# A two-layer transformer block with experts on one core: layer 0's second routing and layer 1's weight fold move into the first expert blocks

## What is computed

```
x = x + tanh(g_xattn[0]) * xattn0(layernorm(x), ctx)          # 16 heads
x = x + tanh(g_ffn[0])   * ffn0(layernorm(x))                 # layer 0's experts:
    scores = softmax(xt @ Wg + bg);  topk_probs, topk_idx = top_k(scores, 2)
    h  = gelu(xt @ W1[e] + b1[e]);   eo = h @ W2[e] + b2[e]
    out = sum over the two experts of topk_probs * eo
x = x + tanh(g_xattn[1]) * xattn1(layernorm(x), ctx)          # 1 head, causal
x = x + tanh(g_ffn[1])   * ffn1(layernorm(x))                 # experts pick tokens
```

## Time and profile before

| | |
|---|---|
| time, 3 runs | median 1029.1 us (1027.45 to 1030.93) |
| the profiled execution | 1028.68 us, of which 1026.9 us are the span of the trace |
| PE | 913.3 us busy, 89% of the span |
| DVE, ACT, POOL | 605.3, 532.7 and 680.3 us busy |
| granted TensorE clock, mean | 0.966 of full speed |

### The profile page before, as it was taken

The page is one execution under the profiler, slowest core; times in us unless marked ns, Lnnn a source line. Parts: engine busy times, 40 slices in busy tenths (PEclk is TensorE's granted clock), DMA queues, the critical chain, the costliest instruction groups (busy, mean ns, idle before and its releaser), DMA issues.

```text
span 1026.9 us, 24961 instructions
## 1 busy us (share of the span) xinstructions
PE 913.3 (89%) x8860; PEld 765.9 (75%) x8860; DVE 605.3 (59%) x1600; ACT 532.7 (52%) x1258; POOL 680.3 (66%) x905
## 2 busy tenths in 40 slices
PE   5999997797739999999999989978998999999991
PEld 3777775565528989999989978865776767778881
DVE  6888889987964563245625769984635324433320
ACT  2666765465415446444644666635555445545440
POOL 6565657588747777376427777721786658878885
PEclk9999999899869999999999999998999999999996
DMA  9364433022145756676456663131364644575454
GB/s 370 119 204 162 154 128 124 17 74 67 51 171 178 216 174 203 209 214 190 157 180 190 196 239 105 58 111 43 53 85 47 114 47 51 84 102 56 50 57 44
DMA packets 130154, 130.73 MB, mean 127 GB/s; under 512 B 32882, under 2 KB 102770, under 8 KB 129138
## 3 DMA queue, kind: packets, MB, share of 16 engines
q1 hardware_dynamic: 99810, 91.69, 28.3%
q0 software_dynamic: 28928, 29.91, 18.2%
q10 hardware_dynamic: 1296, 7.54, 1.8%
HBM read 53.88 MB, written 49.62 MB: 101 GB/s over the span
## 4 chain that ended last, share of the span: by engine, by line
PE 50%; DVE 13%; DMA 13%; POOL 9%; issue 9%; ACT 3%; SPq 1%; POOLq 0%; ACTq 0%; DVEq 0%
PE psum L851 10%; PE psum L861 10%; PE psum L1019 5%; PE psum L1029 5%; DMA odd<-ln_sb,dest 5%; DMA out_x<-ln_sb,dest 4%; PE psum L657 3%; POOL work L1972 2%; PE psum L644 2%; PE psum L674 2%; POOL odd L2046 2%; POOL out_x L2046 2%; DVE w_sb L1169 2%; DVE mx L1163 2%; PE psum L983 2%
## 5 line engine op out<-in xcount | busy, mean ns | idle before, releaser
L1772 ACT ACTIVATE hid_sb<-psum,work 128x128 f32<-128x128 f32 (+1 forms) x424 | 145.6, 412 | 139.2 <-PE psum L851 137.0
L1972 POOL DMA_INDIRECT work<-yg,place x128 | 123.0, 961 | 73.9 <-issue 48.8
L851 PE MATMUL psum<-work 128*128 128x128 f32 (+1 forms) x848 | 150.1, 320 | 2.5 <-issue 2.3
L861 PE MATMUL psum<-w_sb,hid_sb 128*128 x1192 | 150.2, 275 | 0.0
L861 PEld LDWEIGHTS psum<-w_sb,hid_sb 128*128 128x128 f32 x1192 | 144.8, 192 | 2.1
L2046 POOL DMA_INDIRECT out_x<-ln_sb,dest x68 | 105.9, 1558 | 44.5 <-DVE ln_sb L1593 25.1
L1019 PE MATMUL psum<-work,w_sb 128*128 128x272 f32 (+2 forms) x512 | 130.6, 396 | 5.0 <-ACT ctx_sb L1874 3.1
L851 PEld LDWEIGHTS psum<-work 128*128 128x128 f32 x848 | 124.4, 192 | 11.2 <-issue 4.2
L1874 ACT ACTIVATE ctx_sb<-psum,w_sb 128x272 f32<-128x272 f32 (+2 forms) x256 | 116.0, 488 | 25.6 <-PE psum L1019 21.9
L1029 PE MATMUL psum<-ctx_sb,w_sb 128*128 128x272 f32 (+2 forms) x512 | 128.1, 392 | 0.0
L2046 POOL DMA_INDIRECT odd<-ln_sb,dest x68 | 105.7, 1554 | 32.5 <-issue 17.1
(11 more groups left out here) (242 smaller groups left out, 1667.2 us busy)
## 6 DMA issues: line engine op xcount, KB each, us to landing
work<-w_sb SPq DMA_DIRECT2D x76, 322.0 KB, 2.8
work<-xg SPq DMA_DIRECT2D x73, 128.0 KB
yg<-yg_sb SPq DMA_DIRECT2D x73, 128.0 KB
xg<-yg_sb SPq DMA_DIRECT2D x24, 384.0 KB, 4.1
ctx_sb<-tok SPq DMA_DIRECT2D x8, 1088.0 KB, 6.6
ctxn<-sums_sb SPq DMA_DIRECT2D x64, 64.0 KB, 2.0
out_x<-x_sb SPq DMA_DIRECT2D x16, 256.0 KB, 2.1
odd<-yg_sb SPq DMA_DIRECT2D x10, 384.0 KB, 3.0
```

Source lines behind the costliest of these rows:

```text
L851: e.matmul(banks[UP_BANKS[c]][:, 0:cols], w1g(b)[:, c * P:c * P + P], xgT_sb[:, u % 2, at:at + cols], start=True, stop=True).then_inc(s_up, 1)
L861: ins = e.matmul(banks[DOWN_BANKS[b % 2]][:, n * D:n * D + D], hid0[:, b % 2, c, n * P:n * P + P], w2_sb[:, bass.ds(number, 1), c, :].rear ...
L1772: e.activation(hid0[:, b % 2, c, 0:cols], banks[UP_BANKS[c]][:, 0:cols], ACT.Gelu, bias=w1g(b)[:, HID + c:HID + c + 1]).then_inc(s_hg, 1)
L1972: e.indirect_dma_start(dst[:, k, :], None, yg_dram[h], at).then_inc(s_get[i], 16)
```

## The change

In attention the second `route0` no longer runs all its steps from p = 29 on: steps A, B and C run at the ends of passes 31, 32 and 33, the other nine in the expert blocks, three in block 0, two each in blocks 3, 4 and 5 (`ROUTE_STEPS`). The third routing follows it in blocks 6 to 20. The multiplications of the fold move behind the attention products of pass 33, the rest of it into blocks 0 and 1. One half of `w2` and the first block's weights are loaded one pass before the end of attention, in front of SP's transfers of that pass. PSUM banks are given out anew for this. The diff, cut to its core:

```diff
-UP_BANKS, DOWN_BANKS = (0, 1, 2, 5), (3, 6)
+UP_BANKS, DOWN_BANKS = (0, 1, 2, 5), (6, 3)
...
+ROUTE_STEPS = {0: 3, 3: 2, 4: 2, 5: 2, 6: 1, 8: 1, 9: 1, 10: 1, 11: 1, 12: 1, 15: 1, 16: 1, 17: 1, 18: 1, 19: 1, 20: 1}
+SOFTMAX_AT = 7
+COUNT_AT = (2, 14)
...
             for p in range(NP):                        # SP
+                if p == NP - 2:
+                    load_down(0)
+                    w.wait_ge(s_sc, NP)
+                    w.wait_ge(s_kx, NG)
+                    fetch_weights(0)
                 move_sums(p)
...
             for p in range(NP + 3):                    # PE
...
                     attend(p - 2)
+                if p == NP + 1:
+                    multiply_weights()
...
-                if p == NP + 1:
-                    output_bias(1, wo1_sb[:])
-                    multiply_weights()
-                if p == NP + 2:
-                    multiply_bias()
...
-            w.wait_ge(s_x1, NP)
-            w.wait_ge(s_lg, NP)
-            w.wait_ge(s_fs, 2)
+            w.wait_ge(s_rden, NP)
             turn0(0)
...
-                if b == 9:
-                    count0(NPARTS - 1)
+                if b == 1:
+                    multiply_bias()
+                    output_bias(1, wo1_sb[:])
+                if b in COUNT_AT:
+                    count0(1 + COUNT_AT.index(b))
                 if b > 0:
                     down0(b - 1, number)
...
-                for h in range(NPARTS - 1):            # DVE
-                    if p == routing_start(h):
-                        side, begun = route0(h), p
-                steps = ROUTE[p - begun] if 0 <= p - begun < len(ROUTE) else (0, 0, 0)
+                if p == NP - 1:
+                    side = route0(1)
+                steps = ROUTE[p - routing_start] if 0 <= p - routing_start < len(ROUTE) else (0, 0, int(NP - 1 <= p < NP + 2))
...
-                if p == NP + 1:
-                    w.wait_ge(s_put[0], 32 * (PARTS[0][1] // 4))
-                    spread_bias(vec("bv_layer1"))
-                    output_bias(1)
-                    w.wait_ge(s_bias_row, 3)
-                    step.done(e.tensor_scalar(tbo_sb[:], tbo_sb[:], TGX[1], None, ALU.mult))
-                    fold_weights()
-                if p == NP + 2:
-                    fold_bias()
                 for t in range(rows_by(p - 1), rows_by(p)):
                     put_rows(t)
...
-            side = route0(NPARTS - 1)
             rows = later_rows(PARTS[1][0], NT)
+            copy_tokens(0)
+            w.wait_ge(s_put[0], 32 * (PARTS[0][1] // 4))
+            spread_bias(vec("bv_layer1"))
+            fold_weights()
             for _ in range(TG):
                 next(rows)
-            copy_tokens(0)
...
+                if b == 1:
+                    fold_bias()
+                    output_bias(1)
...
                 if h == 0:
-                    if b == 2 or 4 <= b <= 8 or b >= 10:
-                        next(side, None)
+                    for _ in range(ROUTE_STEPS.get(b, 0)):
+                        if next(side, True):
+                            side = route0(NPARTS - 1)
+                            next(side)
```

More of the change, by code:

```diff
@@ L421, in wait_load @@
                 w.wait_ge(ld["xc1" if g == 1 else f"xc{2 + min(g // 4, 2)}"], 32)
-        def routing_start(h):
-            return 2 * (sum(PARTS[h]) // TG - 1) + 7
+        routing_start = 2 * (PARTS[0][1] // TG - 1) + 7
         def part_of(t):
@@ L478, in move_sums, with fetch_weights, load_down @@
                     e.dma_start(ctxn[64 * a:64 * a + 64, i, :], sums_sb[0:P:CHANNELS, i, 2 * P * a:2 * P * a + 2 * P]).then_inc(s_vc[i], 16)
+            def fetch_weights(b):
+                _, h, j, _, _ = BLOCKS[b]
+                w.wait_ge(s_expert, h + 1)
+                number = e.value_load(expert[0:1, h, j:j + 1], min_val=0, max_val=NE - 1)
+                w.wait_ge(ld["w1"], 16 * NE)
+                w.wait_ge(s_hg, HC * (b - NW + 1))
+                w.wait_ge(s_yb, b - NW + 1)
+                e.dma_start(w1g(b), w1_sb[:, bass.ds(number, 1), :].rearrange("p a n -> p (a n)")
+                            ).then_inc(s_w1g[b % NW], 16)
+            def load_down(i):
+                w.wait_ge(s_pt, 4 * (NP - 1 + i))
+                half = slice(i * NE // 2, (i + 1) * NE // 2)
+                load("w2", w2_sb[:, half], t_in["w2a"][:, half])
             filling = fill()
             for p in range(NP):
+                if p == NP - 2:
[3 more added lines that the diff above has]
+                    fetch_weights(0)
                 move_sums(p)
@@ L520, in store_results @@
                 e.dma_start(rows, yg_sb[:, u % 3, 0:n, :]).then_inc(s_yg[u % 3], 16)
-            w.wait_ge(s_sc, NP)
-            w.wait_ge(s_kx, NG)
-            for b in range(AHEAD):
+            load_down(1)
+            for b in range(1, AHEAD):
                 fetch_weights(b)
[L526 to L529, removed]
             for u in range(3):
@@ L591, in output_bias @@
             def output_bias(layer, weights):
+                at = BIAS_COLS[layer]
                 w.wait_ge(s_bv, layer + 1)
-                wait_bank(BIAS_BANKS[layer])
-                e.matmul(banks[BIAS_BANKS[layer]][:, 0:D], ln1[:, 0, :], weights, start=True, stop=True).then_inc(s_bm, 1)
-                free[BIAS_BANKS[layer]] = s_bias_row, 2 * layer + 1
+                e.matmul(banks[BIAS_BANKS[layer]][:, at:at + D], ln1[:, 0, :], weights, start=True, stop=True).then_inc(s_bm, 1)
             def turn(i, bank, s_in, s_done, s_evac, g):
@@ L858, in down0 @@
                 w.wait_ge(s_yb, b - 1)
+                if b == 0:
+                    w.wait_ge(s_x1, NP)
+                    w.wait_ge(s_lg, NP)
+                if b == 1:
+                    w.wait_ge(s_fs, 2)
+                    w.wait_ge(s_bias_row, 3)
                 for n in range(cols // P):
@@ L1312, in vector_program @@
             ROUTE = ((0, 0, 1), (0, 1, 1), (1, 1, 1), (0, 0, 1), (1, 1, 1), (1, 1, 1))
-            side, begun = iter(()), NP + 3
+            side = route0(0)
             for p in range(NP + 3):
-                for h in range(NPARTS - 1):
-                    if p == routing_start(h):
-                        side, begun = route0(h), p
-                steps = ROUTE[p - begun] if 0 <= p - begun < len(ROUTE) else (0, 0, 0)
+                if p == NP - 1:
+                    side = route0(1)
+                steps = ROUTE[p - routing_start] if 0 <= p - routing_start < len(ROUTE) else (0, 0, int(NP - 1 <= p < NP + 2))
                 if p < NP:
@@ L1730, in scalar_program @@
                 g = p // 2 + 1
[L1731 to L1734, removed]
+                if p == routing_start + 1:
+                    for _ in softmax8(*PARTS[0], 0):
+                        pass
                 if 0 <= p - 2 < NP:
@@ L1749, in scalar_program @@
                     output_logits(p - 3)
-                for h in range(NPARTS - 1):
-                    if p == routing_start(h) + 3:
-                        copy_counts(h)
+                if p == NP:
+                    turned_weights()
+                    for _ in softmax8(*PARTS[1], 1):
+                        pass
+                if p == routing_start + 3:
+                    copy_counts(0)
                 if p % 2 == 0 and g < NG:
```

64 lines of the change are left out of this document (29 added, 35 removed).

## The result

The changed kernel takes 1033.72 us (median of 20 runs, 1030.06 to 1036.4), the kernel before 1029.1 us (20 runs, 1023.05 to 1032.3): the ratio is 1.0045, 95% interval 1.0034 to 1.0056. It is slower by 4.6 us, 0.2 us outside the range and on the other side of the 0.3% bound. The profiled execution (1030.85 us, span 1029.0) is among the fastest of its kernel, so its distance to the profiled execution of before, 2.1 us of span, understates the change.

What follows compares the result with a forecast made beforehand. PE bounds the kernel, with the gap between attention and experts to be won, but later puts bind. A 5.3 us lead becomes +0.4 at the first gather; plus 1.4 for the clock over 1028.68 gives 1030.5 us, range 1025.0 to 1033.5.

Steps and rivals of the forecast that it cites:

- First turn at 298.0: Start of the expert blocks: POOL alone sets the pace, so PE's first turn starts at 298.0 instead of 308.10.
- Lead of 5.3 us behind the first blocks: Blocks 0 to 5: of 10.1 us won, 1.4 of added PE work and waits of 2.1 and 1.3 are lost.
- Places at 327.7, first put at 328.0, last put at 428.3: Second routing's addresses ready at 327.7; POOL's put queue for the later parts starts at 328.0, 17.3 us later than before.
- Last put lands 2.23 us after its start, first gather at 430.7: End of POOL's put queue: last put starts at 428.3 and lands at 430.6, then the first gather follows.
- PE's turn at +0.4, idle 5.6 us: At `combine(0)` in part 1: PE's turn at 435.6 instead of 435.25, after some 5.6 us idle; the lead is gone.
- So it does not wait again: Behind `combine(0)`: gathers every 2.5 us, DVE wants at most four tiles in 11.2 us, so no further wait.
- 1.4 for the clock: PE behind its idle stretch at `combine(0)`: one loss of 1.4 us at the lower clock, bounds 0 and 2.9.
- The sum: Whole kernel: 0.4 + 1.4 = 1.8 us above the profiled execution's 1028.68, so 1030.5.
- Rival 1: First gathers: addresses done by about 322 keep the lead, 1023.4 us; 3 us sooner without clock loss, 1025.6; chance 0.20.
- Rival 2: Blocks 0 to 4: DVE waits delay the addresses, each going into the end in full; 3 us gives 1033.5; chance 0.14.
- Rival 3: End of attention: early weight loads hold up attention's transfers; 7 us of hold-up adds 3, 1033.5; chance 0.08.
- rival 4: End of attention: the change opens no gap, POOL's puts being at their own pace by 274.30; excluded by 8.63 us idleness.

Runs made afterwards that it cites:

- the two profiles: The changed kernel's profiled execution (span 1029.0 us) and one from running it unaltered once more (span 1031.6 us; that run measured 1033.81 us, ratio 1.0056).
- filler at the stall: The changed kernel with 11 matmuls of constants, results unused, where PE stands idle behind `combine(0)`: 1034.96 us, ratio 1.0065 to the kernel before.
- its own experiment: The changed kernel with the early weight loads put back behind attention's transfers: 1033.48 us, ratio 1.0047 to the kernel before.
- the places earlier: The changed kernel with the second routing's places one block earlier (three steps each in blocks 3 and 4, none in 5): 1033.19 us, ratio 1.0056.
- the combine one block later: The changed kernel with part 0's first combine four blocks behind part 1's start instead of three: 1030.24 us, ratio 1.0024.
- the fold alone: Fold and early weight loads as changed, both routings where the kernel before has them: 1242.4 us, ratio 0.9991 on the slow chip; 1027.85 us, ratio 0.9981 again elsewhere.
- the other three: On the slow chip, the changed kernel with second-routing places earlier, weight loads at their old place, or a clock filler: 1271.11, 1270.96 and 1270.44 us.
- the first of the four traces: Slow-chip trace of the changed kernel with the second routing's places one block earlier: 1271.11 us, ratio 1.0201.

## Why the prediction was wrong

The mechanism was right, place by place: a lead at the start, a put queue without a gap, DVE's in-order wait at `combine(0)`, PE's stand of 5.9 us and the lower clock behind it. What failed is the price from the last put to the end of the stall. The last put's landing was taken at 2.23 us and measured 3.84 and 3.88 (point 4), and the loss behind PE's turn was taken at 1.4 us and measured 1.9 and 2.6 (point 6), of which PE's restart was priced at nothing.

1. *First turn at 298.0.* 296.72 and 298.41 in the two profiles. POOL's pace of 1.27 us set it, as forecast. The start of this batch differs between executions (272.92 and 274.69 us, and up to 277.52 in the experiments), and everything up to the first gather with it.
2. *Lead of 5.3 us behind the first blocks.* 3.9 and 3.0 at the stall. The waits of the routing's blocks cost what I had said: PE stands only 0.20 and 0.98 us, but counted by its turns the shift goes from -8.6 to -5.3 between 315.54 and 334.03, 3.4 us for 2.1 + 1.3, since every turn that waited has a restart behind it. What I had too small is ahead of it, 2.7 us for 1.4: two up-products ran at the half clock and not one (3.62 and 2.78 us, where I counted 3.3 and 1.8). And the third routing, which I took as costing what it did, cost 1.4 us more (one wait is 0.82 us at 378.33). The lead does not enter the sum: while the puts bind, the lead only sets how long PE stands, as the prediction says.
3. *Places at 327.7, first put at 328.0, last put at 428.3.* 327.18, 327.97 and 428.37 in the first profile; 328.08, 328.88 and 429.23 in the second, which is near its kernel's median (1033.4 us): **0.9 us late there, at slope one.**
4. *Last put lands 2.23 us after its start, first gather at 430.7.* 432.21 and 433.11: the gather started 3.84 and 3.88 us behind the start of the last put. **Mis-sized by 1.5 us**, since I took the landing from a put with no other transfer beside it. The trace names SP's store of results, issued at 429.62, as the releaser. The gather itself waits for stores of part 0, which were issued at 422.61 or before; so I read it as the put's landing beside a weight load (issued at 428.44), a token load and that store. In the five executions of the experiments in which the put itself is named, it took 3.03 to 3.14 us; in the five in which a store is named, the two profiles among them, 3.72 to 3.89. What makes the landing longer is argued, not tested; that it is longer is measured in all ten.
5. *PE's turn at +0.4, idle 5.6 us.* +2.1 and +3.1 (points 3 and 4, and 0.3 us in the gather and the copy); idle 5.85 and 5.88.
6. *"So it does not wait again", and 1.4 for the clock.* Behind the turn 1.9 and 2.6 us were lost (the next turn comes 5.60 and 6.35 us later, for 3.73). Two things make this up. One is the restart, which I had priced at nothing: the up-product starts 0.77 us behind the turn that waited, and 0.22 behind one that did not (442.99 and 443.21), so 0.55 us. It is no matter of the clock, since it is 0.80 us where the clock stayed full (filler at the stall). The other is the lower clock itself: 1.3 us in the first profile, 2.1 in the second, for 1.4. PE in the second:

```profile
438.31 0.66 PE L848 MATMUL psum<-ident,work 128*128 128x128 f32 x2 [5.88 <-DVE work L1361]
439.08 3.75 PE L858 MATMUL psum<-work 128*128 128x256 f32 x8
442.62 2.21 PE L874 MATMUL psum<-w_sb,hid_sb 128*128 x16
```

   "It does not wait again" is false as it stands: DVE waited 0.92 and 0.91 us for tile 1. That cost PE nothing, as its up-product ran meanwhile. But the slack is small. My check by the average (four tiles in 11.2 us against 10 us of gathers) does not see that a queue that starts empty is judged slot by slot: the third slot wants two tiles, and with the clock kept it had about 0.6 us to spare (my estimate), which tile 3's landing of 4.1 us used up.
7. *The sum.* +1.8 forecast. Behind the stall the first profile has +4.0, the second +5.7 (0.4 + 0.9 + 1.5 + 0.3 + 2.6), and the medians differ by 4.6. By the spans, 1.9 us come back between 520 us and the end in the first profile and 1.0 in the second. I did not look into why, so the agreement of the two shifts with the medians is in part luck.

Rival 1 (gathers in time) was out: the places came 0.5 us early or 0.4 late, not 5 early. Rival 2's slope of one is confirmed (+3.4 us for 3.7), but its case, places later than forecast by 1.3 us and more, did not happen. Rival 3 is out by its own experiment, rival 4 by the first turn.

## What to carry to other kernels

A change that closes a gap on one engine often moves a queue on another. Here 10 us won at the start were real, and an in-order wait 130 us later turned them into a loss; the cure was to move the *consumer* (one number, 3 to 6) and not to hurry the producer. Before pricing such a wait, list slot by slot when each item is wanted and when it lands, from an empty queue, with the spread of the landing and not its best value; the mean pace says nothing of the first slots. And where several costs hang on one wait, taking away one of them may show nothing: remove the wait.

## What the runs showed of the hardware

- Whether a pause lowers TensorE's clock is not fixed by its length alone. After 2.01 us of idleness the granted clock was 0.91 in 440 to 460 us with the places earlier, and after 2.00 us it was 1.00 with the combine one block later. Windows of the two kernels, in this order:

```profile
440.00:460.00 20.00, 19.63 (x124) 18.15 (x123) 8.37 (x23) 8.68 (x20) 15.12 (x17) 0.91 0.62 183
```

```profile
440.00:460.00 20.00, 19.68 (x134) 18.39 (x135) 9.12 (x26) 8.54 (x20) 15.12 (x17) 1.00 0.71 199
```

- The landing of the same kind of indirect transfer spread from 2.5 us (tile 0's gather) to 4.1 us (tile 3's) within 10 us of one execution (filler at the stall).
- Behind a turn that had waited for its copy, the next product started 0.77 us after the turn's start at the half clock (the changed kernel) and 0.80 at the full one (filler at the stall); 0.22 us at the full clock where the turn had not waited.
- One chip ran the kernel before and the fold alone 21% slower and the other three 23%, with idleness of PE that no semaphore explains (158 us in the first of the four traces, up to 12.0 at a time).
